# A decay-attention loop: weighted scores times values by column halves, issued behind the next slot's scores

## What is computed

```python
q = elu_plus_one(x @ Wq); k = elu_plus_one(x @ Wk); v = x @ Wv        # 16 heads of 64
a = sigmoid(x @ Wa + ba + 2.0)                                        # one decay per head and token
def step(carry, inp):                                                 # over the 1024 tokens
    S, z = carry
    S = at * S + kt[:, None] * vt[None, :]
    z = at * z + kt
    return (S, z), (qt @ S) / (qt @ z + EPS)
out = out.transpose(0, 2, 1, 3).reshape(b, n, P) @ Wo
```

## Time and profile before

| what | before |
|---|---|
| median of 3 runs | 1127.65 us (1125.08 to 1128.02) |
| profiled execution, first to last instruction (its span) | 1122.8 us |
| what lies around the span | 4.85 us from the span to the median |
| PE busy over the span | 1011.2 us (90%), 9920 matmul records |
| DVE, ACT, POOL busy over the span | 749.8, 749.3 and 437.6 us (67%, 67%, 39%) |
| the decay loop, from the first `across_chunks` to the last `within_chunk` | 664.6 to 961 us |
| records of L1783 (`within_chunk`) | 512, of L1763 (`scores`) 512 (64 groups each) |
| TensorE clock in the loop | 1.00 of full |

### The profile page before, as it was taken

The page is one execution under the profiler, slowest core; times in us unless marked ns, Lnnn a source line. Parts: engine busy times, 40 slices in busy tenths (PEclk is TensorE's granted clock), DMA queues, the critical chain, the costliest instruction groups (busy, mean ns, idle before and its releaser), DMA issues. The chain is left out here.

```text
span 1122.8 us, 26279 instructions
## 1 busy us (share of the span) xinstructions
PE 1011.2 (90%) x9920; PEld 695.7 (62%) x9920; DVE 749.8 (67%) x1513; ACT 749.3 (67%) x1513; POOL 437.6 (39%) x580
## 2 busy tenths in 40 slices
PE   5889999999999999748999789999999999589993
PEld 3333333333333334538999668787888888479993
DVE  7789999999998997882333545656565656433333
ACT  4658888888888887445665577675766666446663
POOL 3742112211122211217764134544444444257751
PEclk9879999999999999968999989999999999779997
DMA  2332111111111100711111422121211110011113
GB/s 72 108 119 87 31 31 51 38 31 30 31 44 45 31 2 3 224 39 48 48 49 41 153 72 76 38 77 38 77 38 76 39 69 9 30 45 49 48 41 127
DMA packets 40034, 64.67 MB, mean 58 GB/s; under 512 B 10024, under 2 KB 21032, under 8 KB 37992
## 3 DMA queue, kind: packets, MB, share of 16 engines
q1 hardware_dynamic: 31736, 50.14, 13.9%
q0 software_dynamic: 4992, 10.23, 3.3%
q10 hardware_dynamic: 3184, 2.63, 0.7%
HBM read 47.86 MB, written 14.68 MB: 56 GB/s over the span
## 5 line engine op out<-in xcount | busy, mean ns | idle before, releaser
L802 ACT ACTIVATE PB<-S 128x512 f32<-128x512 f32 x576 | 307.9, 597 | 71.8 <-PE S L608 67.0
L908 DVE TENSOR_REDUCE mx<-S 128x2 f32<-128x1024 f32 (+1 forms) x192 | 207.5, 1127 | 6.7 <-PE S L594 6.7
L870 POOL TENSOR_SCALAR_AFFINE_SELECT PB<-PB 128x512 f32<-128x512 f32 x128 | 79.0, 635 | 307.4 <-ACT PB L802 307.3
L643 PE MATMUL PV<-PB,VP 128*32 128x256 f32 (+2 forms) x2432 | 177.7, 379 | 0.0
L1526 DVE TENSOR_TENSOR m_hs<-m_gs,m_UP 128x512 f32<-128x512 f32 x78 | 53.7, 688 | 159.6 <-ACT m_gs L1362 157.5
L608 PE MATMUL S<-W 50*128 50x512 bf16 (+3 forms) x768 | 124.0, 329 | 4.9 <-ACT PB L802 4.2
L594 PE MATMUL S<-W 48*128 48x512 bf16 (+3 forms) x640 | 94.4, 326 | 13.0 <-DVE mx L904 4.9
L1202 POOL DMA_INDIRECT yd_rows<-m_ys,m_target x78 | 76.6, 982 | 60.2 <-DVE m_ys L1533 60.2
L643 PEld LDWEIGHTS PV<-PB,VP 128*32 128x32 f32 x2432 | 51.6, 108 | 69.2 <-issue 59.5
L1196 POOL DMA_INDIRECT m_xs<-xn_rows,m_source x78 | 75.8, 972 | 45.5 <-issue 23.1
L594 PEld LDWEIGHTS S<-W 48*128 48x128 bf16 x640 | 26.8, 94 | 107.2 <-issue 45.1
(11 more groups left out here) (315 smaller groups left out, 1965.6 us busy)
## 6 DMA issues: line engine op xcount, KB each, us to landing
d_LQ<-l_rows SPq DMA_DIRECT2D x15, 1024.0 KB, 4.6
W<-qk_parts SPq DMA_DIRECT2D x210, 32.0 KB
qk_parts<-OT SPq DMA_DIRECT2D x24, 256.0 KB, 3.0
W<-qk_parts SPq DMA_DIRECT2D x30, 96.0 KB
W<-in_L_ffn_w_gate SPq DMA_DIRECT2D x1, 2048.0 KB, 10.0
W<-in_L_ffn_w_up SPq DMA_DIRECT2D x1, 2048.0 KB, 15.0
xn_rows<-m_XN SPq DMA_DIRECT2D x8, 256.0 KB, 2.3
m_GB<-yd_rows SPq DMA_DIRECT2D x8, 256.0 KB, 6.4
```

The source lines that it names most:

```text
L643: ins = nc.tensor.matmul(PV[32 * u:32 * u + 32, shift + col:shift + end], VP[:, g, kb, u // 2, :], PB[:, slot, col:end], start=(kb == 0 an ...
L802: nc.scalar.activation(PB[:, j % NPB, :], S2[:, j % 3, :], ACT.Exp, scale=SC).then_inc(exp_done, 1)
L870: nc.gpsimd.affine_select(out=tri, in_=tri, compare_op=ALU.is_ge, fill=0.0, base=0, pattern=[[0, U], [1, P]], channel_multiplier=-1).then_ ...
L908: nc.vector.reduce_max(mx[:, g % 2, c, :, heads[0], qb], S1[:, b, :, 0:w], AX.X)\
```

## The change

Three edits, all in the decay loop. In `within_chunk` each matmul with 128 stationary columns becomes two with 64, one for each half of the columns (and so of the output partitions), with the same moving operand. In the slot on PE, `scores(i + 1)` comes ahead of `within_chunk(i)`. On DVE `weigh(t, i + 1)` comes ahead of `combine(t, b, i)` for the slots 0, 1 and 2. Slot 3 keeps its order on DVE (`combine`, `reciprocals`, `weigh` of the next step).

```diff
--- before.py
+++ after.py
@@ -1780,8 +1780,10 @@
                     pe.wait_ge(w_done, t * 4 + (i + 1))
                     for j in range(4):
                         h = 4 * i + j
-                        last = nc.tensor.matmul(OI[:, j * VW:(j + 1) * VW], WB[:, i % 2, j % 2, j // 2], V1[:, b, h, :],
-                                                start=True, stop=True)
+                        for q0 in (0, 64):
+                            last = nc.tensor.matmul(OI[q0:q0 + 64, j * VW:(j + 1) * VW],
+                                                    WB[:, i % 2, j % 2, j // 2, q0:q0 + 64], V1[:, b, h, :],
+                                                    start=True, stop=True)
                     last.then_inc(intra_done, 1)
 
                 def state(t, b, c):
@@ -1806,11 +1808,11 @@
 
                 def slot(t, b, i, last=False):
                     across_chunks(t, b, i)
-                    within_chunk(t, b, i)
                     if i < 3:
                         scores(t, b, i + 1)
                     elif not last:
                         scores(t + 1, 1 - b, 0)
+                    within_chunk(t, b, i)
 
                 def step(t, b, last=False):
                     first = isinstance(t, int) and t == 0
@@ -2151,22 +2153,22 @@
                 def step(t, b, last=False):
                     first = isinstance(t, int) and t == 0
                     n, nb = t + 1, 1 - b
+                    weigh(t, 1)
                     combine(t, b, 0)
-                    weigh(t, 1)
                     if t >= 2:
                         statistics(t - 2)
                     if not first:
                         update(t - 1, 1)
                     if not last:
                         elu_keys(n, nb)
+                    weigh(t, 2)
                     combine(t, b, 1)
-                    weigh(t, 2)
                     update(t, 0)
                     if t >= 2:
                         moments(t - 2)
                         choose(t - 2)
+                    weigh(t, 3)
                     combine(t, b, 2)
-                    weigh(t, 3)
                     if not last:
                         elu_queries(n, nb)
                     if t >= 2 and (t - 2) % 4 == 3:
```

## The result

| | before | after |
|---|---|---|
| median | 1126.81 us (4 runs, 1125.08 to 1128.02) | **1118.45 us** (4 runs, 1116.94 to 1121.39) |
| ratio to before | | 0.9938 (95% interval 0.9914 to 0.9963) |
| span of the profiled execution | 1122.8 us | 1119.6 us |
| `across_chunks(0)` of step 1 to that of step 15 | 267.95 us | 258.49 us |
| a plain step in it (most of them; see below) | 19.00 us | 18.34 us |

The forecast was 1118.5 us, faster. The hit to the tenth is luck: the runs spread over 4 us, and the forecast counted from 1127.65, where the median of before is 1126.81 now that a fourth run is in it. What can be held against the forecast is the loop itself.

What follows compares the result with a forecast made beforehand. PE looked like the bound, its seam between steps hanging on the queries. Fourteen middle steps gaining 0.75 us (10.5), less 0.65 at each end, gave -9.2, from 1127.65 to 1118.5 us; range 1113.0 to 1126.5.

Steps and rivals of the forecast that it cites:

- The seam hangs on the queries: Where one step meets the next, PE waits for `weigh`, a fixed time after the queries; only gains ahead of them count.
- A group of products in halves costs what `state` costs: In `within_chunk` on PE: a group in halves takes 0.62 us instead of 0.93, or 1.09 together with `state`.
- The rival of halves that don't pair: In `within_chunk`, the two halves run one after the other, 0.93 or more per group: 1131.9 us, chance 0.10.
- A change of shape costs 0.09: On PE, each new change of the array's shape costs 0.09 us, so `across_chunks` takes 0.53 before the scores.
- The wait ahead of `across_chunks(2)`: PE waits 0.29 us for `combine(1)`, behind `weigh(2)` and POOL's mask, plus 0.10 for the restart.
- `weigh(3)` and `combine(2)` behind the mask: On DVE before `across_chunks(3)`: `combine(2)` behind `weigh(3)` doesn't hold it; through at 829.29, `across_chunks(3)` at 829.81.
- The wait ahead of slot 3's scores: PE waits 0.40 us for `elu_queries(0)` before the next step's scores, with the products of slot 3 queued behind.
- they begin with a change of shape, so a restart adds nothing: Scores on PE, 0.65 us per group: no extra restart cost after a wait, where other restarts are put at 0.10.
- The ends lose: Steps 0 and 15 each get 0.65 us longer, with `combine(0)` behind a late `weigh(1)` and `combine(3)` later behind `weigh(3)`.
- The sum: Whole kernel: -10.5 from 14 middle steps, +0.65 for step 0, +0.65 for step 15, so -9.2 us.
- The 4.85 us "around the span": Time added to the profiled execution's span to bring it to the median: 1122.8 to 1127.65, forecast 1113.6 to 1118.5.
- The rival in which the mask line doesn't move with the keys: ACT or POOL is held otherwise, so `combine(1)` lets PE go at 825.74 still: step gains 0.20, 1126.2 us, chance 0.20.

## Why the prediction was right, step by step

- **The seam hangs on the queries.** Right, and the step that carried the sum. The halves alone gained 0.86 per step, the 0.85 that slots 0 to 2 give ahead of the queries. That the old order in slot 3 took 0.44 of waiting from PE and gained 0.12 shows the same from the other side. A sum of PE's savings (four times 0.31) would have given 1.24 per step.
- **A group of products in halves costs what `state` costs.** Right: 0.61 to 0.62 where full width follows, and 1.08 with `state` (forecast 1.09). The rival of halves that don't pair falls: in every step whose timeline is shown the groups have that pace. Its price was too low, though: the order with full-width products, which it put 4.2 above before, was measured 9 to 10 above.
- **A change of shape costs 0.09.** Right on the side that entered the sum: `across_chunks` went from 0.44 to 0.54. The price behind it, 0.10 more in the next group, was missing; the full change doesn't pay it a second time, the order alone does. The Trainium skill (TensorEngine Tiling (Array Packing), Key Properties) says that a change of tiling mode drains TensorE. The timelines of before and of the order alone agree, and these are the numbers for it here. The halves alone pay 0.10 there too (in that kernel the products start 0.54 behind every `across_chunks` but the one at the seam), so it is no cost of the order.
- **The wait ahead of `across_chunks(2)`.** Right in place, cause and size: in the changed kernel it starts 0.29 late (827.59 would follow the turned outputs at 827.10 by 0.49), and without DVE's swap it doesn't wait. `weigh(3)` and `combine(2)` behind the mask cost nothing, as said. No row gave the 0.05 that the sum has for the signal from `combine` to PE; it measured 0.06 (827.82 to 827.88).
- **The wait ahead of slot 3's scores.** Right in place and cause, mis-sized by 0.10. The step that failed is "they begin with a change of shape, so a restart adds nothing": `elu_queries(0)` ends at 832.73 + 0.69 = 833.42 and the scores start 0.14 later, at 833.56, where the sum had 0.03, a term for which it showed no row. So the period is 18.34 and not 18.25, and PE, not `weigh`, sets the seam by a hair. Fourteen times 0.09 is 1.3 us, and the middle steps fell short by 1.0: 9.46 (267.95 - 258.49) of 10.5.
- **The ends lose.** Step 0 lost 0.77 where the clock stayed (17.65 against 16.88), forecast 0.65. From step 15's `across_chunks(0)` to its `combine(3)` it was 12.93 against 12.32, so 0.61, forecast 0.65. In the first profile step 0 lost another 1.61 by the clock (0.45 in `state`, 1.16 in the values), which no step of the prediction had.
- **The sum.** Forecast 9.2. The loop to `combine(3)` is 9.46 - 0.77 - 0.61 = 8.1 shorter, and 6.5 where the clock fell. The medians' 8.4 and 9.8 and the ratios' 7.0 to 10 lie around it. The 4.85 us "around the span" cancels out of the forecast; where span and time of the same execution are both recorded, it is 1.8 (1121.39 - 1119.6), so by an estimate from these numbers the profiled execution of before was some 3 us shorter than the median.
- **The masks.** The rival in which the mask line doesn't move with the keys falls: `weigh(2)` is 5.62 behind the keys' start in both profiles (824.19 - 818.57, 826.33 - 820.71).

## What to carry to other kernels

When an engine is 99% busy and its steps repeat, look for the one place per step where it waits, and follow that wait back: here savings ahead of the point where the chain branches off counted in full (0.86 for the halves of slots 0 to 2), and those behind it not at all. A reordering has to be costed for what it queues: here `combine` behind a mask cost 0.38 us a step (18.34 against 17.96), on an engine that was a third idle, where the halves alone gave 0.86. And where a change bundles several edits, one edit's cost can hide in another's gain: here the order on DVE cost time that the halves more than made up. Running the parts one by one found a kernel 11.9 us faster than the whole.

## What the runs showed that I had not expected

- A wait for a semaphore costs about 0.10 at the restart even where the group begins with a change of shape, and so with loads that start no earlier than its matmuls (both at 837.32, where nothing waits): it is 0.14 to 0.15 from the producer's end to the scores' start, in three kernels (0.44 idle each).
- A change of the array's shape costs on both sides, 0.10 at the end of the one group and 0.10 in the first interval of the next: a full-width group of 8 records cost 1.03 between two others in the kernel with the order alone, 0.93 behind another full-width group in the kernel before.
- In one of three profiles of the changed kernel the granted clock fell to 0.50, its lower level, for some 3.4 us, 1.8 us behind the end of an idle time of 1.64 us on PE, and cost 1.6 us; in the other two the same idle time was followed by a clock of 1.00. What made the difference isn't known.
- On one chip of those used before took 1182 us where it took 1127 on the others, while the changed kernel's loop was as long as on another chip to 0.03 us. The extra time lies outside the loop: in the changed kernel the loop began 28 us later there (698.12 against 669.81), and what follows its last products took 188 us in place of 159.
